# Attention scores as float32 products on 32-row strips instead of bf16 parts on 96 rows

## What is computed

```
x: (4, 512, 256) float32; w_qkv: (256, 768); 16 heads of 16
qkv = x @ w_qkv;  q = q / 4
scores = q . k per head, causal mask, softmax over the keys
out = (attn @ v) @ w_out
x = layernorm(x + out)
```

## Time and profile before

| | |
|---|---|
| median of 3 executions | 408.42 us (408.01 to 408.6) |
| profiled execution | 409.33 us, span of its instructions 407.6 us |
| mean granted clock of TensorE | 0.987 |
| busy, TensorE / its weight loads | 372.9 / 222.1 us |
| busy, VectorE / ScalarE / GpSimd | 291.8 / 241.6 / 236.9 us |
| moved by DMA | 74.78 MB |

### The profile page before, as it was taken

How to read it: one execution, slowest core, us unless ns; L and a number is a source line. 1 busy time by engine, 2 the same in 40 slices (tenths; PEclk the granted TensorE clock), 3 DMA queues, 4 the chain that set the end, 5 groups by cost and what they waited for, 6 DMA issues and landing times.

```text
span 407.6 us, 10397 instructions
## 1 busy us (share of the span) xinstructions
PE 372.9 (91%) x2894; PEld 222.1 (54%) x2894; DVE 291.8 (72%) x1009; ACT 241.6 (59%) x534; POOL 236.9 (58%) x374
## 2 busy tenths in 40 slices
PE   5989999999999999998989899999999999999570
PEld 2535555444565546663544457676677776775130
DVE  1258777997899989989899489866566666661663
ACT  2422567767556776557857447665566665667642
POOL 5422254434323798427882764777777777776581
PEclk9989999999999999999999999999999999999996
DMA  4859464757851293749648454646565555528893
GB/s 134 258 183 272 133 205 158 208 133 220 234 161 45 70 274 116 206 141 275 191 153 236 136 164 118 185 147 196 178 185 161 165 159 174 174 57 317 325 378 115
DMA packets 54071, 74.78 MB, mean 183 GB/s; under 512 B 9842, under 2 KB 45308, under 8 KB 52480
## 3 DMA queue, kind: packets, MB, share of 16 engines
q1 hardware_dynamic: 46832, 56.93, 49.0%
q0 software_dynamic: 6912, 16.93, 11.4%
q10 hardware_dynamic: 272, 0.26, 0.2%
HBM read 46.33 MB, written 29.66 MB: 186 GB/s over the span
## 4 chain that ended last, share of the span: by engine, by line
PE 51%; POOL 13%; issue 12%; DVE 11%; DMA 6%; SPq 2%; ACT 2%; DVEq 0%; POOLq 0%; ACTq 0%
POOL scratch_y L1783 12%; PE PS L868 9%; PE PS L821 8%; PE PS L847 7%; PE PS L790 6%; PE PS L697 3%; DMA XP<-scratch_y 3%; PE PS L804 3%; PE PS L928 3%; PE PS L719 2%; PE PS L898 2%; DMA scratch_qk<-PA 2%; PE PS L665 1%; PE PS L878 1%; DVE PS L1432 1%
## 5 line engine op out<-in xcount | busy, mean ns | idle before, releaser
L1139 ACT ACTIVATE PT<-PS 128x512 f32<-128x512 f32 x160 | 91.3, 596 | 36.8 <-PE PS L847 32.4
L1783 POOL DMA_INDIRECT scratch_y<-Y,XG x80 | 80.5, 1006 | 26.1 <-issue 20.4
L1755 POOL TENSOR_SCALAR_AFFINE_SELECT PT<-PT 128x256 f32<-128x256 f32 (+1 forms) x140 | 50.3, 369 | 71.6 <-ACT PT L1139 69.6
L1774 POOL DMA_INDIRECT scratch_slots<-XP,RI x64 | 63.9, 998 | 34.9 <-issue 16.2
L1432 DVE CUSTOM_DVE_ANT_0 PS<-PS,mneg 128x512 f32<-128x512 f32 (+1 forms) x138 | 67.6, 533 | 15.5 <-PE PS L821 15.2
L821 PE MATMUL PS<-KS,QS 96*128 96x512 bf16 (+3 forms) x256 | 61.6, 302 | 2.3 <-DVE MX L1430 0.8
L847 PE MATMUL PS<-QS,KS 98*128 98x512 bf16 (+3 forms) x256 | 61.0, 300 | 2.6 <-ACT PT L1139 1.8
L697 PE MATMUL PS<-W,XGT 128*64 x320 | 60.5, 332 | 0.7 <-DVE WG L1289 0.3
L699 PE MATMUL PS<-WG,XGT 128*64 128x192 f32 x320 | 60.6, 332 | 0.0
L1353 DVE SCALAR_TENSOR_TENSOR HH<-PS,XG,SG 128x96 f32<-128x96 f32 x80 | 25.0, 317 | 33.0 <-ACT SG L1061 31.0
L697 PEld LDWEIGHTS PS<-W,XGT 128*64 128x64 f32 x320 | 40.5, 136 | 12.6 <-issue 8.3
(11 more groups left out here) (235 smaller groups left out, 695.7 us busy)
## 6 DMA issues: line engine op xcount, KB each, us to landing
XG<-scratch_slots SPq DMA_DIRECT2D x160, 65.0 KB
scratch_qk<-PA SPq DMA_DIRECT2D x14, 384.0 KB, 3.7
W<-in_gate_up_dram SPq DMA_DIRECT2D x16, 288.0 KB
KS<-scratch_qk SPq DMA_DIRECT2D x32, 128.0 KB, 3.7
YL<-scratch_y SPq DMA_DIRECT2D x8, 512.0 KB, 6.7
QS<-scratch_qk SPq DMA_DIRECT2D x8, 384.0 KB, 4.1
QS<-scratch_qk SPq DMA_DIRECT2D x24, 128.0 KB, 3.9
W<-in_down_dram SPq DMA_DIRECT2D x8, 288.0 KB
```

The source lines that it names most:

```text
L1139: e.activation(PT[:, p % NPT, n, :], PS[:, 2 + (rank[u] - 1) % 2, :], ACT.Exp).then_inc(st_exp, 1)
L1755: e.affine_select(out=d, in_=d, compare_op=ALU.is_ge, fill=0.0, base=0, pattern=[[0, 1 if n < 2 else 2], [1, 128]], channel_multiplier=-1) ...
L1774: e.indirect_dma_start(out=XS[:, :], out_offset=bass.IndirectOffsetOnAxis(ap=RI[:, b % 2, TOPK * q + n:TOPK * q + n + 1], axis=0), in_=XP[ ...
L1783: e.indirect_dma_start(out=YK[:, :], out_offset=bass.IndirectOffsetOnAxis(ap=XG[:, j % NXG, D + 1:D + 2].bitcast(I32), axis=0), in_=Y[:, j ...
```

## The change

The scores become float32 products. Two heads lie in a strip of 32 rows, as two sets: in set 0 the rows 0 to 15 of a strip hold head 0 and the others zeros (Q) or ones (K), in set 1 the other way round. ScalarE writes both sets straight from the PSUM bank of the projection, with a scale and a bias for each row (`QC`, made by seven small VectorE steps at the start). A strip belongs to a pair, four pairs fill 128 rows; the host orders the columns of w_qk for it. The negated maximum is one float32 row in the idle half of the strip. QS and KS are four groups deep. Max and st units take slots in turn from two pairs, so that four units in a row (max and st of one pair, max and st of the next) lie on four different strips. The parts, the residual, the scratch in DRAM, the rows of ones, `keep_busy` at the start and the mask products of the max units go. Misc units stand behind slots 1, 3, 6 and 8 of ten, at most two at each; the projections and values of the first batches and the loads of the experts' weights have other slots.

```diff
-RG = 3
+RG = 4
+MISC_AT = (1, 3, 6, 8)
-WEIGHTS = ((0, 3, 75), (3, 3, 80), (6, 3, 134), (9, 3, 137), (12, 3, 140), (15, 4, 143), (19, 3, 145), (22, 3, 160),
-           (25, 3, 163), (28, 4, 165))
+WEIGHTS = ((0, 3, 75), (3, 3, 80), (25, 3, 90), (28, 4, 95), (6, 5, 134), (11, 3, 138), (14, 4, 142), (18, 3, 148),
+           (21, 4, 162))
...
+    plan += [("qk", 0, 0), ("qk", 0, 2)]
+    early = [("qk", 0, 1), ("qk", 0, 3), ("v", 0, 0), ("v", 0, 1), ("xg", 0), ("qk", 1, 0), ("qk", 1, 2), ("v", 1, 0),
+             ("qk", 1, 1), ("v", 1, 1), ("qk", 1, 3), ("xg", 1)]
+    for n, u in enumerate(early):
+        put((1, 3, 6, 8, 11, 13, 16, 21, 23, 26, 28, 31)[n], u)
...
-            if i < PAIRS:
-                plan.append(("max", i, u))
-            if 0 <= i - LAG < PAIRS:
-                plan.append(("st", i - LAG, u))
+            v = slot % 10
+            pair, n = slot // 10 * 2 + v % 2, v // 2
+            if pair < PAIRS:
+                plan.append(("max", pair, n))
+            if 0 <= pair - LAG < PAIRS:
+                plan.append(("st", pair - LAG, n))
...
-            run_slot(slot, 1)
+            run_slot(slot, 2 if v in MISC_AT or i >= PAIRS else 0)
...
+def strip_of(i):
+
+    return (i + 2 * (i // 4)) % 4
...
-                    e.wait_ge(ld_in[r], 144 * (g // RG + 1))
-                    for h, qt, c0 in pair_scores(n, 2 * (i % 4), 3, 2, 1):
+                    if i % 4 == 0 and n < 2:
+                        for m in (g % 2, 2 + g % 2):
+                            if n == 0:
+                                e.wait_ge(first_set, rank["qk", g // 2, m])
+                            else:
+                                e.wait_ge(*free(("qk", g // 2, m)))
+                    for o, qt, c0 in pair_scores(n, 0, 3, 2, 1):
                         w = 128 * (qt + 1)
-                        t = e.matmul(PS[:, kk, c0:c0 + w], QS[r][0:96, h, 128 * qt:128 * qt + 128],
-                                     KS[r][0:96, h, 0:w], start=(c0 == 0), stop=not mask_by_product(i, n),
-                                     skip_group_check=True)
+                        t = e.matmul(PS[:, kk, c0:c0 + w], QS[r][at:at + 32, o, 128 * qt:128 * qt + 128],
+                                     KS[r][at:at + 32, o, 0:w], start=(c0 == 0), stop=True, skip_group_check=True)
...
-                        t = e.matmul(PS[:, kk, c0:c0 + w], KS[r][0:98, h, 128 * j:128 * j + 128],
-                                     QS[r][0:98, h, 128 * j:512], start=(c0 == 0), stop=True,
+                        t = e.matmul(PS[:, kk, c0:c0 + w], KS[r][at:at + 32, o, 128 * j:128 * j + 128],
+                                     QS[r][at:at + 32, o, 128 * j:512], start=(c0 == 0), stop=True,
...
-                    e.activation(PA[:, r, 0, :], PS[:, k, :], ACT.Copy,
-                                 scale=0.25 if m < 2 else 1.0).then_inc(part0, 1)
-                elif kind == "part":
+                    if rank[u] == 1:
+                        e.wait_ge(scales, 7)
+                    wait_st_group(e, g - RG)
+                    for o, signal in enumerate((first_set, done)):
+                        e.activation(to[:, o, :], PS[:, k, :], ACT.Identity, bias=QC[:, 6:7] if m < 2 else QC[:, 4 + o:5 + o],
+                                     scale=QC[:, o:o + 1] if m < 2 else QC[:, 2 + o:3 + o]).then_inc(signal, 1)
...
-                if kind == "resid":
...
-                    for h, qt, c0 in pair_scores(n, h0, 3, 2, 1) if n < 4 else ():
+                    for o, qt, c0 in pair_scores(n, 0, 3, 2, 1):
                         w = 128 * (qt + 1)
-                        if mask_by_product(i, n):
-                            t = e.tensor_reduce(M[:, h, qt:qt + 1], PS[:, kk, c0:c0 + w], AX.X, ALU.max)
-                        else:
-                            t = e.tensor_tensor_reduce(PS[:, kk, c0:c0 + w], PS[:, kk, c0:c0 + w],
-                                                       mneg[:, S - w:S], 1.0, LOWEST, ALU.add, ALU.max,
-                                                       M[:, h, qt:qt + 1])
+                        t = e.tensor_tensor_reduce(PS[:, kk, c0:c0 + w], PS[:, kk, c0:c0 + w], mneg[:, S - w:S], 1.0,
+                                                   LOWEST, ALU.add, ALU.max, M[:, 2 * o + i % 2, qt:qt + 1])
```

More of the change, by code:

```diff
@@ L80, in follow @@
         plan.append(u)
[L81 to L85, removed]
+        if u[0] == "sendmax":
             put(slot + 2, ("nmout",) + u[1:])
@@ L124, in run_slot @@
             follow(slot, entry[1])
[L126 to L132, removed]
-        else:
[L134 to L152, removed]
+    plan += [("qk", 0, 0), ("qk", 0, 2)]
[3 more added lines that the diff above has]
+        put((1, 3, 6, 8, 11, 13, 16, 21, 23, 26, 28, 31)[n], u)
+    for b in range(2, B):
+        for n, m in enumerate((0, 2, 1, 3)):
+            put(20 * (2 * b + n // 2) - 28 + 5 * (n % 2), ("qk", b, m))
+        for c in range(2):
+            put(VALUES_AT[b - 2] + 2 * c, ("v", b, c))
+    put(18, ("xt", 2))
+    put(44, ("xt", 3))
     for b in range(B):
@@ L159, in make_plan @@
     put(27, ("wog",))
-    for b in range(1, B):
-        put(5 * (8 * b - 2) + 4 if b == 1 else VALUES_AT[b - 2] + 5, ("xg", b))
+    for b in range(2, B):
+        put(VALUES_AT[b - 2] + 5, ("xg", b))
     for lo, n, slot in WEIGHTS:
         put(slot, ("w", lo, n))
-    for g in range(2, 2 * B):
-        put(5 * (4 * g - 3), ("load", g))
     for g in range(PAIRS // 2):
@@ L370, in build @@
         xt_in = [[sem(f"xt_in{b}_{c}") for c in range(2)] for b in range(B)]
[L371 removed]
+        wv_in, wo_in, gt_in, spare_in = (sem(n) for n in ("wv_in", "wo_in", "gt_in", "spare_in"))
+        scales, first_set = sem("scales"), sem("first_set")
         wq_in = [sem(f"wq_in{n}") for n in range(4)]
@@ L429, in wait_st_group, with wait_dead @@
                 e.wait_ge(st_full, 20 * (g + 1))
+        def wait_dead(e, lo, n):
+            for start, end, last in tenants:
+                if start >= base + (lo + n) * WROW * 4 or end <= base + lo * WROW * 4:
+                    continue
+                if last == "inputs":
+                    for m in range(4):
+                        e.wait_ge(*full(("qk", B - 1, m)))
+                    for v in range(2):
+                        e.wait_ge(*full(("v", B - 1, v)))
+                    e.wait_ge(*full(("xg", B - 1)))
+                elif last == "values":
+                    wait_pv(e, 8 * (B - 1) - 1)
+                else:
+                    wait_st_group(e, last)
         def wait_pv(e, p):
@@ L539, in _ @@
                     e.dma_start(X[:, 4 * b:4 * b + 4, :], xr[:, 4 * b:4 * b + 4, :]).then_inc(x_in[b], 16)
[L540 to L567, removed]
                 elif kind == "small":
@@ L1397, in _ @@
             weights_step, found = {}, {}
+            wait_const(e, "idf")
+            by_strip = idf[:, :].rearrange("p (a c) -> p a c", c=32)
+            for n, (lo, hi) in enumerate(((0, 16), (16, 32))):
+                e.tensor_reduce(QC[:, 2 + n:3 + n], by_strip[:, :, lo:hi], AX.XY, ALU.add).then_inc(scales, 1)
+                lo = 16 - lo
+                e.tensor_reduce(QC[:, 4 + n:5 + n], by_strip[:, :, lo:lo + 1], AX.XY, ALU.add).then_inc(scales, 1)
+            e.memset(QC[:, 6:7], 0.0).then_inc(scales, 1)
+            e.wait_ge(scales, 5)
+            for n in range(2):
+                e.tensor_scalar(QC[:, n:n + 1], QC[:, 2 + n:3 + n], 0.25, None, ALU.mult).then_inc(scales, 1)
             wait_const(e, "iot")
```

125 lines of the change are left out of this document (34 added, 91 removed).

## The result

The changed kernel takes 491.15 us (488.55 to 493.86, 4 runs) against 408.51 us of the kernel before in the same comparison: a ratio of 1.203, interval 1.196 to 1.210. It is 83 us slower. The forecast was 443: the sign was right, the size was not half of it. The time lies at the price of the rival "two deep" by chance: the reason is another, as the rows will show. Executions of one kernel can lie some per cent apart, the longer ones at a lower granted clock, so kernels are compared by the executions within 1.5% of their fastest.

A forecast was written before the change was run, and what follows sets the result against it. TensorE was taken to bound attention. Start -3, slots 20 to 159 +36, last slots +8 and hidden waits -6 sum to +35 us: median 443 us, own range 430 to 457, wider range 408 to 494.

The forecast's parts named there:

- two deep: Rival for attention's score groups: a strip queues one running and one waiting pass, so split units block others; 493 us, chance 0.20.
- third slot of a group: In three-slot score groups, the third S waits for its bank until 1.71 us; the group takes 2.71 us.
- one by one: Rival for score groups: a unit starts only when the previous unit's last pass has started; 531 us, chance 0.05.
- loads in a row: Rival for score groups: row strips cannot load weights side by side, +28 us; 471 us, chance 0.12.
- bank free: Rival for three-slot groups: the third S does not wait for its exp, group 1.86 us; 410 us, chance 0.10.
- faster: Rival: the earlier first S decides, with strips never empty and banks never waited for; 398 us, chance 0.10.
- the tail: Slots 160 to 179, S units alone: grouped units 15.5 us plus masks 2.2 make 17.7 us; +8 us.
- the clock: TensorE's granted clock: no term in the sum; a fall below 1.00 was listed as a sign of being wrong.
- the new gaps: Where a granted clock below 1.00 would show the prediction wrong; it had averaged 0.92 from 22.44 to 44.82 us.
- the tens: Attention's runs of ten slots, 20 to 159: scores +36 us, 7 us of work moved from the start, waits -6.
- 14 x 7.4: Score time of slots 20 to 159: 14 tens, each two groups of 1.00 and two of 2.71 us.
- the -6 for old waits: Slots 20 to 159: longer runs of ten slots hide part of 11 us of existing waits; -6 us taken.

The follow-up runs named there:

- h_before_add: Kernel before with one more bf16 product of 512 columns ahead of each max unit from the fifth pair on: 432.41 us against 409.05.
- j_three_banks: Changed kernel with a third PSUM bank for st units, taken from the misc units: two executions at 507.25 and 508.26 us, two at 519.38 and 521.02.
- c_two_slots: Changed kernel with misc units behind slots 1, 3, 5, 7 and 9 and the third PV piece behind slot 5: 467.48 us.
- b_tail_fill: Changed kernel with two unread bf16 products of 128 rows and 512 columns behind each of the last 20 st units: 487.41 us.
- a_tail_pool: Changed kernel with the masks of the last four pairs made by GpSimd instead of a full-height TensorE product: 480.73 us.
- k2_strip_fill: Changed kernel with two unread 32-row products behind each of the last 20 st units: 558.91 us, on a chip where the kernel before took 472.99.
- by-pair order: Changed kernel with five slots of one pair, then five of the next, so two strips alternate instead of four: six executions, 511.76 to 544.32 us.

## Why the prediction was right and wrong

**Right.** TensorE bounds attention (h_before_add, in the kernel before). A float32 unit holds its strip for four times the bf16 time, and four strips work at once (1.07 us for a group of two slots, forecast 1.00). The first max unit came at 10.63 us (forecast 10.7). The third slot of a group pays for the exp of its bank: shown by j_three_banks (2.93 to 2.03 us) and by c_two_slots (28 us over 15 tens). All these are the forecast's mechanism. Of the rivals, two deep and one by one fell with the rows at 142.65 us, loads in a row with the overlapping loads there, bank free with the third S at 133.92, and faster with the sign. Two deep, by its own sum 443 + 52 = 495 and not 493, met the time by luck. That the lighter load of VectorE and of the DMA queues buys nothing was not tested by itself.

**Wrong: the tail, +8 forecast, +29 measured.** The step read "three groups of two (1.0), three of three (2.7) and one of five", "plus masks 2.2". It took groups, and the masks as 0.11 us each, and overlooked what the masks are: full-height work, which by the prediction's own rule ends a group. Thus there are 20 units one by one, 1.27 or 1.11 us each, in place of groups. With the clock at full rate the tail would be about 30 us (b_tail_fill without its fillers), 6 more than the 24 of the forecast (16 and 8); with the masks taken from TensorE (a_tail_pool) it would be 24.

**Wrong: the clock, 0 in the sum.** It was named only as a sign of being wrong, and there for "the new gaps"; in the tail it fell where TensorE had no gap. There it costs 15 us, half of the 29. Over the whole span the mean granted clock is 0.938 of 492.1 us against 0.987 of 407.6: 30.5 us less than full against 5.3. The difference, 25 us, is the most that it can have cost, since not all of the span waits for TensorE. Three further dips lie before the tail: 28 to 31 us, 184 to 192 and 242 to 250.

**Mis-sized: the tens, +37 forecast, +60 measured.** The runs of score units from the first st unit to the last max transpose, each from its first unit to the next other work, add up to 127 us in the timeline, where the sum had 14 x 7.4 = 104. The other work of that stretch takes 99 us, and the forecast's terms (166 - 67 before, + 7 - 6) give 100. So nearly all of the miss lies in the groups, and the -6 for old waits is in keeping with this. All these are estimates from the start times of one execution:
- Of 21 three-slot groups, those without a projection take 2.93 us in place of 2.71. The prediction counted the opening of a strip once, 0.14 us at the end of a group; the first S pays 0.11 for it too, and the bank's period is 1.86 us.
- Eight of them take 3.15, because a projection's two copies stand before the exp on ScalarE. The prediction named these copies ("as before, 0.6 each") and put them at no cost. Together the 21 groups are 7 us over the sum.
- The groups of two slots take 1.07 or little more, 1 to 2 us over.
- Four times nothing was due behind slot 8, and the groups of two and three ran into one of five slots. Such a group takes 4.74 us at 65.44, 77.44 and 105.58 us, and 5.27 at 170.96; the sum had 3.71. That is 5 us, and no term of the prediction asked whether the break would be there.
- The rest, some 10 us, lies in nine other groups, many of them at or near the dips from 184 and from 242 us, which took at most 7 us together. One, at 181.69, takes 5.22 us for three slots: two copies and one more ScalarE step of 1.23 us stand before its exp, and the clock falls. The rest was not divided further.

## What to carry to other kernels

In this kernel row strips multiplied TensorE's rate only while all four were filled: each full-height product between them, a mask or a filler too, closed the group, and the price was the strip time of all that ran alone. So list, for every group, what ends it, and whether that is really due there. When a unit lives four times as long, work out again when its PSUM bank comes free, from its first pass to the end of its reader, with what stands before the reader on its engine. When TensorE works on one or two strips, look at the granted clock row and not at the busy share.

## What the hardware showed that I had not expected

The granted clock fell to 0.50 while TensorE was busy for 47.60 of 47.60 us, where most of its time went to float32 products on one strip of 32 rows, with full-height ones between. With 40 more full-height products it was 1.00 (b_tail_fill); with 40 more of 32 rows 0.52 (k2_strip_fill, on another chip); with two strips side by side and short waits 0.50 (a_tail_pool). The Trainium skill, "TensorE: Matmul & The Clock Gate", Part 1, puts the low rate down to an idle TensorE; here it also came with a busy one. The dips come at other places in other executions, which spreads the times of one kernel by up to 6% (511.76 to 544.32 us for the by-pair order), while span times clock agreed within 0.3% in its six executions.

On four row strips a later product can start before an earlier one: 142.68 against 143.19 us above.
